# Keys and values projected in one product, squares taken on GpSimd, and routing work moved within its steps

## The reference

```python
x = x + attn(layernorm(x), wq, wk, wv, wo)
x = x + ffn(layernorm(x), w_router, wg, wu, wd, sg, su, sd)

# attn: 32 query heads, 8 key/value heads, head width 8
q, k, v = x @ wq, x @ wk, x @ wv            # 256, 64 and 64 columns
scores = einsum('bhqd,bhkd->bhqk', q, k) / sqrt(8) + amask   # amask: -1e10 where i-128 <= j < i
out = (softmax(scores) @ v) @ wo

# ffn: 8 experts, each token goes to its 2 best; 2 shared experts see all tokens; inner width 640
out = sum_e comb[t, e] * wd_e(silu(wg_e x) * wu_e x) + sum_j sd_j(silu(sg_j x) * su_j x)
```

## Time and profile before

| | us |
|---|---|
| median of 3 runs | 929.55 (927.91 to 929.57) |
| profiled execution, its own time | 928.54 |
| its span, first to last instruction | 926.9 |
| PE busy | 883.4 (95%) |
| ACT busy | 583.1 (63%) |
| DVE busy | 448.1 (48%) |
| POOL busy | 276.4 (30%) |

### The profile page before, as it was taken

The page is one execution under the profiler, slowest core; times in us unless marked ns, Lnnn a source line. Parts: engine busy times, 40 slices in busy tenths (PEclk is TensorE's granted clock), DMA queues, the critical chain, the costliest instruction groups (busy, mean ns, idle before and its releaser), DMA issues.

```text
span 926.9 us, 23991 instructions
## 1 busy us (share of the span) xinstructions
PE 883.4 (95%) x8163; PEld 563.6 (61%) x8164; DVE 448.1 (48%) x769; ACT 583.1 (63%) x733; POOL 276.4 (30%) x423
## 2 busy tenths in 40 slices
PE   8989999999999999999999999999999999999994
PEld 5533333333333333333347888887888999999983
DVE  8634443343444344454547777657843443443432
ACT  4789999999999999999993423342222222222220
POOL 5043334333233433333340000000023544544542
PEclk9979999999999999999999999999999999999998
DMA  5434444655444566632102207100008785565521
GB/s 186 132 114 174 146 161 164 212 206 200 174 138 164 176 212 212 240 97 85 33 13 75 69 19 242 46 2 23 1 27 271 237 249 155 159 188 133 153 35 22
DMA packets 42027, 123.88 MB, mean 134 GB/s; under 512 B 7668, under 2 KB 23028, under 8 KB 35824
## 3 DMA queue, kind: packets, MB, share of 16 engines
q1 hardware_dynamic: 31152, 110.35, 34.6%
q0 software_dynamic: 7072, 9.72, 6.1%
q10 hardware_dynamic: 3744, 3.02, 1.0%
HBM read 74.03 MB, written 49.02 MB: 133 GB/s over the span
## 4 chain that ended last, share of the span: by engine, by line
PE 72%; ACT 11%; DVE 10%; issue 5%; DMA 1%; DVEq 0%; POOLq 0%; POOL 0%; ACTq 0%
PE ps L1714 18%; PE ps L1884 14%; PE ps L1667 14%; PE ps L1838 8%; ACT arena L952 8%; PE ps L1903 7%; PE ps L1851 4%; DVE ps L1176 3%; PE ps L1894 2%; PE ps L1608 2%; PE ps L1769 2%; DVE arena L1311 1%; DVE hsh L1314 1%; ACT hsh L981 1%; PE ps L1865 1%
## 5 line engine op out<-in xcount | busy, mean ns | idle before, releaser
L952 ACT ACTIVATE arena<-ps 128x1024 f32<-128x1024 f32 x336 | 317.0, 1041 | 1.7 <-PE ps L1667 1.6
L1714 PE MATMUL ps<-arena 128*32 128x256 f32 x4096 | 265.6, 386 | 0.9 <-POOL arena L781 0.8
L781 POOL TENSOR_SCALAR_AFFINE_SELECT arena<-arena 128x512 f32<-128x512 f32 x240 | 150.0, 638 | 277.9 <-ACT arena L963 179.6
L1667 PE MATMUL ps<-arena 64*128 64x512 bf16 (+1 forms) x1280 | 184.2, 342 | 14.9 <-ACT arena L952 5.7
L1714 PEld LDWEIGHTS ps<-arena 128*32 128x32 f32 x4096 | 112.3, 109 | 104.2 <-issue 38.8
L1176 DVE COPY_PREDICATED ps<-keep,ps 128x512 f32<-128x512 int32 (+1 forms) x128 | 80.6, 630 | 162.8 <-PE ps L1667 162.8
L1667 PEld LDWEIGHTS ps<-arena 64*128 64x128 bf16 x1280 | 54.0, 94 | 168.1 <-ACT arena L952 80.4
L1884 PE MATMUL ps<-wr_all,x2T 128*128 x648 | 141.3, 362 | 2.1 <-issue 1.0
L963 ACT ACTIVATE arena<-ps 128x1024 f32<-128x1024 f32 x112 | 114.1, 1034 | 7.8 <-DVE ps L1176 2.7
L1884 PEld LDWEIGHTS ps<-wr_all,x2T 128*128 128x128 f32 x648 | 106.6, 189 | 19.5 <-issue 3.9
L1838 PE MATMUL ps<-x2T,wr_all 128*128 128x512 f32 x480 | 117.0, 394 | 1.3 <-issue 1.2
(11 more groups left out here) (191 smaller groups left out, 710.7 us busy)
## 6 DMA issues: line engine op xcount, KB each, us to landing
w_scr<-wr_all SPq DMA_DIRECT2D x24, 1280.0 KB, 7.4
wr_all<-w_scr SPq DMA_DIRECT2D x24, 1280.0 KB, 6.2
raw<-w_experts SPq DMA_DIRECT2D x24, 640.0 KB, 7.5
arena<-q_scr SPq DMA_DIRECT2D x64, 64.0 KB
o_scr<-arena SPq DMA_DIRECT2D x128, 32.0 KB, 1.6
arena<-o_scr SPq DMA_DIRECT2D x16, 256.0 KB, 3.9
raw<-w_shared SPq DMA_DIRECT2D x6, 640.0 KB, 4.5
q_scr<-parts SPq DMA_DIRECT2D x8, 384.0 KB, 2.7
```

Source lines behind the costliest of these rows:

```text
L781: nc.gpsimd.affine_select(out=dst, in_=src, compare_op=ALU.is_ge if own else ALU.is_gt, fill=0.0, base=0, pattern=[[0, REP], [-1 if own el ...
L952: nc.scalar.activation(prob[:, SLOT[unit(a, kt)], :, :].rearrange("p h q -> p (h q)"), score.rearrange("p b x -> p (b x)"), ACT.Exp, scale ...
L1667: return nc.tensor.matmul(ps[:, bank, :].rearrange("p (h q) -> p h q", h=2)[:, :, place * P:(place + tiles) * P], kst[r0:r0 + HALF, s, kt ...
L1714: last = nc.tensor.matmul(ps[32 * h:32 * h + 32, 6 + qc, a % 2 * QW:(a % 2 + 1) * QW], vst[:, s, kt, :], prob[:, SLOT[k], h, :], start=(no ...
```

## The change

Seven edits, in the order of the program:

- wk and wv lie side by side in wkv_sb, so the third projection block has 128 rows, keys below and values (transposed) above. ACT copies the upper half out (vT), and PE turns it with 4 transposes per chunk in place of 8 products. In the last chunk all four come before squared_norms (half of the products came after it).
- POOL squares the high parts (tensor_tensor of a part with itself), ACT no more.
- POOL's fills of vaug and kst start when one chunk is normalised; its keep masks lie before the last chunk's squares.
- The flag is computed from the square of the bound; ACT writes two of the three pieces of kst, DVE three and a copy of a whole row (counts 3 and 3 become 4 and 2).
- In the shared steps `between` comes ahead of the wait for ACT's rounding and L1314; slot_table stays behind them.
- tiles_first moves from step 29 to behind the adds at the end of chunk 2.
- The last tile's transposed hidden rows are copied and split in two pieces, and PE's down products wait for each piece by itself.

```diff
-        wk_sb = carve(KD * KV * HD).rearrange("p (k n) -> p k n", k=KD)
-        wv_sb = carve(KD * KV * HD).rearrange("p (k n) -> p k n", k=KD)
+        wkv_sb = carve(KD * 2 * KV * HD).rearrange("p (k n) -> p k n", k=KD)
...
+        vT = maxjunk[KV * HD:P, :, 0:CT]
...
-            pool.wait_ge(a_xn, 2)
+            pool.wait_ge(a_xn, 1)
             step(nc.gpsimd.memset(vaug[:, :, :, :], 0.0))
...
-            pool.wait_ge(a_xn, NC)
-
+            pool.wait_ge(first_const, N_FIRST)
+
+            def squares_of(c):
+                for m in range(3):
+                    r = P if m < 2 else KV * HD
+                    pool.wait_ge(a_p0, c * 3 + m + 1)
+                    if c >= 2:
+                        pool.wait_ge(a_norm, c - 1)
+                    nc.gpsimd.tensor_tensor(squares[0:r, c % QC, m, :], parts[0:r, c % QC, m, 0, :], parts[0:r, c % QC, m, 0, :],
+                                            ALU.mult).then_inc(a_sq, 1)
+
+            for c in range(NC - 1):
+                squares_of(c)
             for side, own in enumerate((True, False)):
...
-            pool.wait_ge(shift_low, 3)
+            squares_of(NC - 1)
+            pool.wait_ge(shift_low, 4)
...
                     if m == 2:
+                        nc.scalar.copy(vT[:, c % 2, :], ps[KV * HD:P, 4, :]).then_inc(a_vT, 1)
                         between()
-                    act.wait_ge(a_p0, c * 3 + m + 1)
-                    nc.scalar.activation(squares[0:rows(m), qc, m, :], parts[0:rows(m), qc, m, 0, :], ACT.Square) \
-                        .then_inc(a_sq, 1)
...
-            for s, k0, k1 in CONST_ROW:
+            for s, k0, k1 in CONST_ROW[0:2]:
                 nc.scalar.copy(kst[HALF:HALF + 1, s, k0:k1], ps[HALF:HALF + 1, 7, 128:129].to_broadcast([1, k1 - k0])) \
...
-            hT_out(j + 1, 1)
+            act.wait_ge(e_th, j + 2)
+            for i, (k0, k1) in enumerate(LAST_PARTS):
+                nc.scalar.copy(hidT[:, 1, 0, k0:k1].rearrange("p k t -> p (k t)"), ps[:, 4 + i, 0:(k1 - k0) * P]) \
+                    .then_inc(e_hThi, 1)
...
-            dve.wait_ge(u_root, 1)
-            nc.vector.tensor_scalar(norm_row[0:1, 4:5], norm_row[0:1, 3:4], BOUNDED, None, ALU.is_le).then_inc(u_step, 1)
+            dve.wait_ge(u_top, 1)
+            nc.vector.tensor_scalar(norm_row[0:1, 4:5], norm_row[0:1, 2:3], BOUNDED * BOUNDED, None, ALU.is_le).then_inc(u_step, 1)
...
+            dve.wait_ge(u_root, 1)
...
+            dve.wait_ge(shift_high, 2)
+            nc.vector.tensor_copy(kst[HALF:HALF + 1, 1, :], kst[HALF:HALF + 1, 0, :]).then_inc(shift_low, 1)
...
+                    between(step)
                     dve.wait_ge(s_hi, step + 1)
                     nc.vector.tensor_tensor(hsh[:, q % HR, 1, :], hsf[:, q % 2, :], hsh[:, q % HR, 0, :].bitcast(F32),
                                             ALU.subtract).then_inc(s_split, 1)
                     ahead_of(step)
-                    between(step)
+                    if step == TABLE_STEPS[-1]:
+                        slot_table()
...
+                if c == NC - 2:
+                    tiles_first()
...
-                    w = wq_sb[:, :, m * P:(m + 1) * P] if m < 2 else wk_sb
-                    r = P if m < 2 else KV * HD
+                    w = wq_sb[:, :, m * P:(m + 1) * P] if m < 2 else wkv_sb
...
+                    pe.wait_ge(a_vT, c + 1)
                     for t in tiles:
-                        for k in range(KD):
-                            last = nc.tensor.matmul(ps[:, 5, t * 64:(t + 1) * 64], x1T[:, c % 2, k, t * P:(t + 1) * P],
-                                                    wv_sb[:, k, :], start=(k == 0), stop=(k == KD - 1))
+                        last = nc.tensor.transpose(ps[:, 5, t * 64:(t + 1) * 64], vT[:, c % 2, t * P:(t + 1) * P],
+                                                   ident[KV * HD:P, KV * HD:P])
...
-                if c < NC - 1:
-                    value_rows(range(TPC)).then_inc(a_v, 1)
-                    squared_norms()
-                else:
-                    value_rows(range(TPC // 2))
-                    squared_norms()
-                    value_rows(range(TPC // 2, TPC)).then_inc(a_v, 1)
+                value_rows(range(TPC)).then_inc(a_v, 1)
+                squared_norms()
...
-            routed_hT(j + 1, 1)
-            routed_down(j + 1, 1, slot_1)
+            routed_hT(j + 1, 1, lambda k: (4, k) if k < LAST_PARTS[1][0] else (5, k - LAST_PARTS[1][0]))
+            routed_down(j + 1, 1, slot_1, LAST_PARTS)
```

More of the change, by code:

```diff
@@ L232 @@
 HOT = 3
+LAST_PARTS = ((0, 2), (2, KI))
 CONST_ROW = ((0, 0, L // 2), (0, L // 2, L), (1, 0, L))
@@ L402, in build @@
         dve_step, pool_step = sem("dve_step"), sem("pool_step")
-        a_xn, a_tp, a_xT, a_proj, a_v, a_vsb = (sem(n) for n in ("a_xn", "a_tp", "a_xT", "a_proj", "a_v", "a_vsb"))
+        a_xn, a_tp, a_xT, a_proj, a_vT, a_v, a_vsb = (
+            sem(n) for n in ("a_xn", "a_tp", "a_xT", "a_proj", "a_vT", "a_v", "a_vsb"))
         a_p0, a_rem, a_p1, a_p2 = (sem(n) for n in ("a_p0", "a_rem", "a_p1", "a_p2"))
@@ L911, in _ @@
                 .then_inc(x_in[0], 16)
-            for dst, w in ((wq_sb, wq), (wk_sb, wk), (wv_sb, wv), (wo_sb, wo), (wr_sb, wr)):
+            for dst, w in ((wq_sb, wq), (wkv_sb[:, :, 0:KV * HD], wk), (wkv_sb[:, :, KV * HD:P], wv), (wo_sb, wo), (wr_sb, wr)):
                 act.dma_start(dst, w.rearrange("(k p) n -> p k n", p=P)).then_inc(wq_in if w is wq else w_in, 16)
@@ L1513, in routing @@
                     count_tiles_last()
-                if step == 29:
-                    tiles_first()
                 if step == 30:
@@ L1530, in routing @@
                     place_rows(1)
-                if step == 37:
-                    slot_table()
             def up(j, p):
@@ L1574, in _ @@
             y_out(j, 0)
-            hT_low(j + 1, 1)
+            for i, (k0, k1) in enumerate(LAST_PARTS):
+                dve.wait_ge(e_hThi, j + 2 + i)
+                nc.vector.tensor_tensor(hidT[:, 1, 1, k0:k1].rearrange("p k t -> p (k t)"),
+                                        ps[:, 4 + i, 0:(k1 - k0) * P],
+                                        hidT[:, 1, 0, k0:k1].rearrange("p k t -> p (k t)").bitcast(F32), ALU.subtract) \
+                    .then_inc(e_hT, 1)
             y_out(j + 1, 1)
@@ L1607, in _ @@
                     for k in range(KD):
-                        last = nc.tensor.matmul(ps[0:r, 2 + m, :], w[:, k, :], x1T[:, c % 2, k, :],
+                        last = nc.tensor.matmul(ps[:, 2 + m, :], w[:, k, :], x1T[:, c % 2, k, :],
                                                 start=(k == 0), stop=(k == KD - 1))
@@ L1645, in _ @@
             with pe.If(pe.value_load(flag[0:1, 0:1], min_val=0, max_val=1) > 0):
-                pe.wait_ge(shift_low, 3)
-                pe.wait_ge(shift_high, 3)
+                pe.wait_ge(shift_low, 4)
+                pe.wait_ge(shift_high, 2)
                 with pe.Fori(0, NG) as n:
@@ L1888, in routed_up, with routed_hT @@
                 return last
-            def routed_hT(j, p):
+            def routed_hT(j, p, place=lambda k: (4 + k // 4, k % 4)):
                 pe.wait_ge(e_hid, j + 1 + FIRST)
@@ L1893, in routed_hT, with routed_down @@
                 for k in range(KI):
-                    last = nc.tensor.transpose(ps[:, 4 + k // 4, k % 4 * P:(k % 4 + 1) * P],
+                    bank, column = place(k)
+                    last = nc.tensor.transpose(ps[:, bank, column * P:(column + 1) * P],
                                                hid[:, p, k * P:(k + 1) * P], ident[:, :])
                 last.then_inc(e_th, 1)
-            def routed_down(j, p, slot):
-                pe.wait_ge(e_hT, j + 1 + FIRST)
+            def routed_down(j, p, slot, parts=((0, KI),)):
                 pe.wait_ge(e_y, j + FIRST)
+                starts = {k0: i for i, (k0, _) in enumerate(parts)}
                 for k in range(KI):
+                    if k in starts:
+                        pe.wait_ge(e_hT, j + (starts[k] + 1 + FIRST))
                     for w, v in PRODUCTS:
```

## The result

| | before | after |
|---|---|---|
| median of the runs (us) | 929.06 (925.64 to 929.57, 7 runs) | 926.11 (925.35 to 926.76, 7 runs) |
| profiled execution, its own time | 928.54 | 925.88 |
| its span | 926.9 | 924.2 |
| PE busy | 883.4 | 877.8 |
| POOL busy | 276.4 | 289.5 |

What follows compares the result with a forecast made beforehand. PE, busy 95% of the span, was taken as the bound. Shared stage -5.4, prologue +0.4, start -0.6, clock +1.5, end 0 sum to -4.1 from the profiled 928.54: 924.4, range 921.0 to 927.3.

Steps and rivals of the forecast that it cites:

- Shared stage: Routing moved into DVE's wait for ACT: PE's two waits go (2.1 and 1.8 us), clock stays full (1.5); 5.4 less.
- Rival C: Shared stage: the wait moves to step 28's L1314 or ACT's silu queue slips; half of 5.4 lost, 927.1; chance 0.12.
- First chunk: Prologue: POOL's squares run behind its earlier fills and the second blocks DVE's L1077; 0.9 us slower, 0.2 without blocking.
- POOL's square: Prologue: one square on POOL takes 1.2 us, as two reads in turn, between bounds of 0.61 and 1.8.
- Second and third chunk: Prologue: ACT's copies limit the gain to 0.5 us a chunk; blocking between POOL and DVE leaves 0.25 each.
- Clock in the prologue: PE idles 2 to 2.7 us in 4 in the first chunk; one clock fall, 1.5 us more.
- A: Rival: the clock holds in the prologue; 922.9 with blocking, 921.7 without; chance 0.32.
- B: Rival: the clock stays down through the later projections, 5.5 us more for each of three; 939; chance 0.06.
- Start of attention: ACT writes two pieces of kst instead of three, so the first exponential starts 0.6 us earlier; 0.6 less.
- Last tile: Split tile: POOL's last add waits for the landing of the one before, which doesn't move; 0, at best 0.1.

Runs made afterwards that it cites:

- squares_filled: Kernel after with each POOL square replaced by two fills that read nothing, the squares left out of the computation; 925.92 us, ratio 0.9966.
- squares_act_late: Kernel after with the squares back on ACT and POOL's fills again waiting for two normalised chunks; 927.13 us, ratio 0.9987.
- turns_in_gap: Kernel after with transposes of the identity that nobody reads put ahead of the values' transposes in the first three chunks; 924.98 us, ratio 0.9959.
- old_prologue: Kernel before with all of the change but the prologue's edits (shared steps, start of attention, last tile changed); 922.05 us, ratio 0.9928.

## Why the prediction came out as it did

The time fell inside the range and on the forecast side, 1.7 above the forecast. The range's upper end is not worked out in full: a second fall of the clock gives 924.4 + 1.5 = 925.9, and no sum is shown for the other 1.4. By its own steps:

- **Shared stage, -5.4 forecast, -5.73 measured.** Right in each part: both waits gone, step 29's multiply at the moment given, 641.03, as ACT's silu ended (640.40 + 0.60; DVE came free in the same moment, 641.04), clock 1.00. The largest term and the best founded, since each link had a row. Rival C is out.
- **First chunk, +0.9 forecast, +3.34 measured.** The term that was mis-sized. Three things failed in it. The fills were put at 8.6, but POOL had an iota ahead of them that waited for a DMA (9.30), so the squares began at 16.88 and not 16.0. Next, nothing was charged for moving the fills across DVE's L1049 and L1056, though the earlier trace rows showed a DVE operation of 128x4 standing until a fill ended; the block was priced for L1077 alone. Measured, the normalised rows of the next chunk are ready at 15.94 for 14.09, 1.85 later. Last, the block behind the squares cost L1077 1.6 where 0.36 was assumed (17.35 to 18.4 against its own 0.69), because it waited for two squares and not one, and it struck the first block's L1077, not the second's; squares_filled gives 1.20 back. With neither early fills nor squares on POOL (squares_act_late) the chunk is 0.7 longer than in before, so these two edits are 2.6 of the 3.3.
- **POOL's square, 1.2 forecast.** 1.03 here (2.05 for two). The Trainium skill's rate (GPSIMD Engine Reference, 3.1) had given 1.1 as an estimate, nearer than my row-based choice.
- **Second and third chunk, -0.25 each, 0 measured.** The third took 8.74 (41.89 - 33.15) for 8.68 in before, and the second takes 8.73 where the clock is full (turns_in_gap). PE waits there for ACT's copy of the values (1.44), the bound that the prediction named and put at 0.5 better than before. What it left out is that ACT comes to the keys' copy 0.43 later in the chunk (39.56 - 33.15 = 6.41 for 34.43 - 28.45 = 5.98). In the trace that delay is there from the start of the chunk: with the copy of vT in ACT's row, DVE's last operation on the keys of the chunk before (L1092, L1077 in before) starts 0.49 into the chunk where it started 0.06 into it (33.64 - 33.15, 28.51 - 28.45), and the chunk's own operations stand behind it.
- **Clock in the prologue, +1.5 forecast, +1.3 measured.** The slow products are 2.1 longer (7.50 less 5.42), but the chunk is only 1.31 longer than the next (10.05 for 8.74), since PE's wait for the values behind them shrank from 1.44 to 0.67; turns_in_gap, without the fall, takes 8.73. One fall, as said, then full speed until the products end; rivals A and B are out for this kernel. But B's mechanism was real in part: squares_act_late has a fall in every chunk. It recovers within each projection, so its price is 1.7 a chunk and not 5.5.
- **Start of attention, -0.6.** The exponentials moved by 0.5, but in the time of whole kernels it isn't to be found (+0.5 by the fit). In after's trace attention gained 0.25 more, which lies within what the clock's return varies.
- **Last tile, 0 forecast, -0.6 measured.** The step that failed is "the add waits for the landing of the one before". I had a coincidence: the landing as the chain draws it (918.03) fell among POOL's own steps from 917.09 to the add at 918.78, and I took the one that doesn't move as the bound. Those steps take 1.69 with and without a landing to wait for.

Sum, by the ledger: errors of +2.4 in the first chunk, -0.2 on the clock, +0.6 in the second and third chunk, +0.1 ahead of the first scores, -0.15 in attention, -0.3 in the shared stage, -0.45 in the routed stage ahead of its last tile (not traced to a cause) and -0.6 at the end give 1.4, the difference between -4.1 and -2.7. That the sum came out as near as it did is in part luck: the terms at the end and in the routed stage, which the forecast put at nothing, took 1.0 off the error of the prologue. The gain came from the shared edit, and 0.6 from the last tile; the prologue's edits cost 4.1 (926.11 against old_prologue's 922.05).

## What to carry to other kernels

When work moves to an idle engine, list which instructions of its neighbour it will now lie beside, the moved fills as well as the new operation, and price each from the one row where such a pair already met. Before taking products off an engine whose clock can fall, ask what else keeps it busy there: dense work that looks like pure cost may be paying for the speed of what follows, and if it must go, transposes that nobody reads are a cheap stand-in (they gave back 3.0 of 5.1 us here; keeping the products was still better). A DMA's end that coincides with the waiting engine's own steps is not evidence that the DMA was the bound; look for the same steps where no DMA was waited for.

## What the runs showed of the hardware

- POOL operations that only write hold up DVE's tensor_scalar with its data in SBUF: 128x4 took 1.04 us in place of 0.17, four of 128x256 took 2.32 in place of 1.38. Three squares, which also read, made the four take 4.74. Operations that only write don't stop a DVE tensor_tensor with two SBUF inputs (0.69 in both cases), which a reading POOL operation does (2.27). The Trainium skill (SBUF — State Buffer, Who interferes with whom) states both: tensor_scalar can take the pair of ports shared with GpSimd in a 2-port mode, and a two-input operation contends only with GpSimd's reads. The lengths agree with both; which mode DVE ran in no trace shows. The prediction drew on the second rule only, for an edit that fell under the first.
- The clock fell in chunks where PE stood for 1.65 and 1.18 us, and even 0.64 and 1.18, with little between (squares_act_late), but not ahead of after's third and fourth projections, where it stood once, 0.67 and 1.44. In squares_filled it did not fall at 0.95 and 0.55, and fell at 1.14 and 0.55. Its full level came back within the projections behind each time (6.62 to 8.22 in place of 5.42).
- A bf16 POOL tensor_tensor of 128x512 takes 1.03 us, and 64 partitions take the same (1.06).
